# Query and key rows laid out in DRAM by pair of batches, with mask, ones and zero rows in blocks of 28

## What is computed

```python
query = seq2 + b_self
key = jnp.concatenate([seq1 + b_prev, seq2 + b_self], 1)
value = jnp.concatenate([seq1, seq2], 1)
q = (query @ Wq + bq).reshape(b, l2, H, DH).transpose(0, 2, 1, 3)
k = (key @ Wk + bk).reshape(b, l1 + l2, H, DH).transpose(0, 2, 1, 3)
...
score_prev = jnp.einsum('bhqd,bhkd->bhqk', q, k[:, :, :l1]) * SCALE
score_self = (q * k[:, :, l1:]).sum(-1, keepdims=True) * SCALE
mask = jnp.arange(l1)[None, :] < seq_len1[:, None]
score_prev = jnp.where(mask[:, None, None, :], score_prev, -jnp.inf)
score = jnp.concatenate([score_prev, score_self], -1)
weights = jax.nn.softmax(score, axis=-1)
```

## Time and profile before

| | |
|---|---|
| median of three runs | 500.7 us (499.92 to 501.67) |
| the profiled execution's own time | 500.33 us |
| its span, first to last instruction | 497.1 us |
| PE busy | 450.9 us (91%) |
| DVE, ACT, POOL busy | 344.3, 267.4, 191.7 us |
| mean granted TensorE clock | 0.943 |
| moved by DMA | 37.31 MB in 44730 packets |
| span's shares in the chain that ended last | PE 59%, DVE 11%, DMA 8%, SP's queue 8% |

### The profile page before, as it was taken

How to read it: one execution, slowest core, us unless ns; L and a number is a source line. 1 busy time by engine, 2 the same in 40 slices (tenths; PEclk the granted TensorE clock), 3 DMA queues, 4 the chain that set the end, 5 groups by cost and what they waited for, 6 DMA issues and landing times.

```text
span 497.1 us, 7804 instructions
## 1 busy us (share of the span) xinstructions
PE 450.9 (91%) x2278; PEld 328.2 (66%) x2278; DVE 344.3 (69%) x634; ACT 267.4 (54%) x544; POOL 191.7 (39%) x187
## 2 busy tenths in 40 slices
PE   6889899789999999999999999999997879978795
PEld 2667678567787887777788776887884434434442
DVE  5398567586777789677778967776875655766562
ACT  2457657465464664546466454646555434545463
POOL 4456676882132533113253311333773121222220
PEclk9689989899999999999999999999999785989889
DMA  5324333220004011000401000032107266455620
GB/s 152 112 79 112 122 86 112 79 67 1 2 7 125 3 63 42 0 0 6 123 2 62 21 1 0 7 104 65 61 22 195 64 176 180 141 168 167 179 74 22
DMA packets 44730, 37.31 MB, mean 75 GB/s; under 512 B 4216, under 2 KB 39196, under 8 KB 44700
## 3 DMA queue, kind: packets, MB, share of 16 engines
q1 hardware_dynamic: 43248, 36.64, 25.4%
q0 software_dynamic: 1024, 0.26, 0.3%
q10 hardware_dynamic: 432, 0.10, 0.1%
HBM read 26.07 MB, written 10.66 MB: 74 GB/s over the span
## 4 chain that ended last, share of the span: by engine, by line
PE 59%; DVE 11%; DMA 8%; SPq 8%; issue 5%; ACT 5%; POOL 3%; ACTq 0%; DVEq 0%
PE acc_ps L550 6%; SPq L460 5%; PE g_ps L550 5%; PE g_ps L552 5%; PE g_ps L551 5%; PE acc_ps L552 5%; PE acc_ps L551 5%; DVE act_lo L1103 4%; DMA w_raw<-in_L_cond_Wu 4%; PE u_ps L550 4%; PE u_ps L552 4%; PE u_ps L551 4%; DVE act_p L1099 3%; PE st_ps L718 3%; PE pv_ps L730 3%
## 5 line engine op out<-in xcount | busy, mean ns | idle before, releaser
L837 ACT ACTIVATE act_p<-g_ps 128x512 f32<-128x512 f32 x144 | 86.1, 598 | 135.4 <-PE g_ps L552 120.2
L1099 DVE TENSOR_TENSOR act_p<-act_p,u_ps 128x512 f32<-128x512 f32 x144 | 98.5, 684 | 72.9 <-PE u_ps L552 45.3
L1103 DVE TENSOR_TENSOR act_lo<-act_p,act_hi 128x512 fp32r<-128x512 f32 x144 | 121.9, 846 | 0.2 <-ACT act_hi L842 0.2
L1305 POOL TENSOR_TENSOR xg_lo<-xg,xg_hi 128x512 fp32r<-128x512 f32 x35 | 50.2, 1433 | 149.4 <-ACT xg_hi L847 149.4
L842 ACT ACTIVATE act_hi<-act_p 128x512 fp32r<-128x512 f32 x144 | 89.8, 624 | 4.8 <-DVE act_p L1099 4.7
L550 PE MATMUL acc_ps<-act_hi,w_split 128*128 128x512 f32 x144 | 62.1, 431 | 15.7 <-DVE act_lo L1103 15.6
L933 ACT ACTIVATE probs_t<-st_ps 128x512 f32<-128x512 f32 x64 | 38.2, 597 | 47.6 <-PE st_ps L718 47.5
L550 PE MATMUL g_ps<-x_hi,w_split 128*128 128x512 f32 (+1 forms) x144 | 58.6, 407 | 1.4 <-DVE x_lo L1128 1.4
L551 PE MATMUL g_ps<-x_lo,w_split 128*128 128x512 f32 (+1 forms) x144 | 57.7, 400 | 0.0
L552 PE MATMUL g_ps<-x_hi,w_split 128*128 128x512 f32 (+1 forms) x144 | 57.6, 400 | 0.0
L550 PE MATMUL u_ps<-xg_hi,w_split 128*128 128x512 f32 x144 | 57.1, 397 | 0.0
(11 more groups left out here) (147 smaller groups left out, 715.9 us busy)
## 6 DMA issues: line engine op xcount, KB each, us to landing
k_blocks<-k_rows SPq DMA_DIRECT2D x32, 96.0 KB
q_plain<-q_rows SPq DMA_DIRECT2D x8, 384.0 KB
q_blocks<-q_rows SPq DMA_DIRECT2D x32, 96.0 KB
k_plain<-k_rows SPq DMA_DIRECT2D x8, 384.0 KB
v_both<-v_d SPq DMA_DIRECT2D x8, 272.0 KB, 3.6
w_raw<-in_L_cond_Wg SPq DMA_DIRECT2D x8, 256.0 KB, 2.9
w_raw<-in_L_cond_Wu SPq DMA_DIRECT2D x8, 256.0 KB, 3.1
w_raw<-in_L_cond_Wd SPq DMA_DIRECT2D x8, 256.0 KB, 2.9
```

Of the source, the lines that this page charges most:

```text
L837: activation(act_p[k % 3][:], g_ps[k % 3][:], ACT.Silu).then_inc(silu_done, 1)
L1099: tt(act_p[k % 3][:], act_p[k % 3][:], u_ps[k % 3][:], ALU.mult).then_inc(prod_done, 1)
L1103: tt(act_lo[k % 3][:], act_p[k % 3][:], act_hi[k % 3][:].bitcast(F32), ALU.subtract).then_inc(act_lo_done, 1)
L1305: tt(xg_lo[e % 3][:], xg[:].rearrange("p b s -> p (b s)"), xg_hi[e % 3][:].bitcast(F32), ALU.subtract)\
```

## The change

The two DRAM tensors become (pair, 112 rows, 4, 256): a pair of batches lies together, and within it four blocks of 28 rows, of which 24 are as before, row 24 is the mask (keys) or ones (queries), and 25 to 27 are zero (for keys; for queries too, behind the ones). Each store of `store_rows` becomes two DMAs, one for each pair, of 128 pieces of 1 KB. Two DMAs of constants (512 and 384 KB, DRAM to DRAM) and four mask DMAs in place of one come behind the first tile. The block tiles put the groups j outermost, so that each block load is 28 partitions of one contiguous 4 KB, and each plain load 112 partitions of 4 KB. The loads of lines 466, 477 and 519 go away. A pair takes 13 DMAs. The matmuls of lines 619 and 718 contract over 112 and 114 rows in place of 97 and 99 and read their columns in steps of 4 KB in place of 1 KB.

```diff
-            def store_rows(dst, tok, places):
+            def store_rows(dst, t, places):
 
-                of_place = dst[0:ROW_MASK].rearrange("(j s r) i n -> j s (r i) n", j=GJ, s=3)
                 his, lo = places
-                for s in his:
-                    sp.dma_start(of_place[:, s, :, tok], rows_hi[:].bitcast(F32)).then_inc(rows_stored, 16)
-                sp.dma_start(of_place[:, lo, :, tok], rows_lo[:].bitcast(F32)).then_inc(rows_stored, 16)
+                for rows, s in [(rows_hi, s) for s in his] + [(rows_lo, lo)]:
+                    for m in range(TB // PAIR):
+                        to = dst[t * (TB // PAIR) + m].rearrange("(j x) i n -> j x i n", j=GJ)[:, s * DH:(s + 1) * DH]
+                        sp.dma_start(to.rearrange("j r i n -> j (r i) n"),
+                                     rows[:, m * PAIR * S:(m + 1) * PAIR * S].bitcast(F32)).then_inc(rows_stored, 16)
...
+            for rows, first in ((q_rows, 0), (k_rows, 1)):
+                to = rows.rearrange("p (j x) i n -> p j x (i n)", j=GJ)[:, :, BLOCK_MASK + first:BLOCK_ROWS]
+                sp.dma_start(to.rearrange("p j x n -> p j (x n)"),
+                             a["row_pads"][first:].rearrange("x n -> (x n)").unsqueeze(0).unsqueeze(0)
+                             .to_broadcast([NP, GJ, (BLOCK_ROWS - BLOCK_MASK - first) * GI * PAIR * S])).then_inc(pads_stored, 16)
             sp.wait_ge(mask_stored, 16)
-            sp.dma_start(k_rows[ROW_MASK:], mask_row.rearrange("b s -> (b s)").unsqueeze(0).unsqueeze(0)
-                         .to_broadcast([1, GI, B * S])).then_inc(later_stored, 16)
+            for j in range(GJ):
+                sp.dma_start(k_rows[:, BLOCK_ROWS * j + BLOCK_MASK],
+                             mask_row.rearrange("(p b) s -> p (b s)", b=PAIR).unsqueeze(1).to_broadcast([NP, GI, PAIR * S]))\
+                    .then_inc(later_stored if j == 0 else mask_stored, 16)
...
-            def load_blocks(dst, src, tok, semaphore):
+            def load_blocks(dst, src, p, semaphore):
 
                 for j in range(GJ):
-                    r = slice(3 * DH * j, 3 * DH * (j + 1))
-                    sp.dma_start(dst[r, :, j].bitcast(F32), src[r, :, tok]).then_inc(semaphore, 16)
+                    r = slice(BLOCK_ROWS * j, BLOCK_ROWS * (j + 1))
+                    sp.dma_start(dst[r, j].bitcast(F32).rearrange("r i n -> r (i n)"),
+                                 src[p, r].rearrange("r i n -> r (i n)")).then_inc(semaphore, 16)
+
+            def load_plain(dst, src, p, semaphore):
+                sp.dma_start(dst[0:ROW_MAX].bitcast(F32).rearrange("r i n -> r (i n)"),
+                             src[p].rearrange("r i n -> r (i n)")).then_inc(semaphore, 16)
...
-                mm((s_ps[i % 2] if bank is None else bank)[:], q_plain[n // 2 % 2][0:ROW_MASK + 1, i, half(n)],
-                   k_blocks[n // 2 % 2][0:ROW_MASK + 1, i, :, half(n)], start=True, stop=True).then_inc(s_written, 1)
+                mm((s_ps[i % 2] if bank is None else bank)[:], q_plain[n // 2 % 2][0:ROW_MAX, i, half(n)],
+                   k_blocks[n // 2 % 2][0:ROW_MAX, :, i, half(n)], start=True, stop=True).then_inc(s_written, 1)
```

More of the change, by code:

```diff
@@ L33 @@
 GI, GJ = 4, 4
-ROW_MASK = 3 * DH * GJ
-ROW_MAX = ROW_MASK + 1
+BLOCK_MASK = 3 * DH
+BLOCK_ROWS = BLOCK_MASK + 4
+ROW_MAX = BLOCK_ROWS * GJ
 Q_SLOTS, K_SLOTS = ((0, 2), 1), ((0, 1), 2)
@@ L46 @@
 NP = B // PAIR
+ROW_STORES = 16 * 3 * TB // PAIR
 NEXT_SLOT = {18: ("side", 0), 20: ("query", 0), 22: ("natural", 0), 24: ("natural", 1), 26: ("natural", 2),
@@ L91, in dram @@
             return nc.dram_tensor(name, shape, F32, kind="Internal").ap()
-        q_rows = dram("q_rows", (ROW_MASK, GI, B * S))
-        k_rows = dram("k_rows", (ROW_MASK + 1, GI, B * S))
+        q_rows = dram("q_rows", (NP, ROW_MAX, GI, PAIR * S))
+        k_rows = dram("k_rows", (NP, ROW_MAX, GI, PAIR * S))
         mask_row = dram("mask_row", (B, S))
@@ L246, in build @@
         mask_stored = sem("mask_stored")
+        pads_stored = sem("pads_stored")
         dif_step, z_step, gate_step, small_cast = sem("dif_step"), sem("z_step"), sem("gate_step"), sem("small_cast")
@@ L393, in later_stores @@
                 sp.wait_ge(aux_drained, n + 3)
-                store_rows(k_rows, bass.ds(t * N, N), K_SLOTS)
+                store_rows(k_rows, t, K_SLOTS)
                 sp.wait_ge(aux_drained, n + 4)
@@ L453, in _ @@
             later_stores(NT - 2)
-            def load_blocks(dst, src, tok, semaphore):
+            def load_blocks(dst, src, p, semaphore):
                 for j in range(GJ):
-                    r = slice(3 * DH * j, 3 * DH * (j + 1))
-                    sp.dma_start(dst[r, :, j].bitcast(F32), src[r, :, tok]).then_inc(semaphore, 16)
-            def load_first(p, m):
[L464 to L469, removed]
-            def load_second(p, m):
[L473 to L478, removed]
+                    r = slice(BLOCK_ROWS * j, BLOCK_ROWS * (j + 1))
[4 more added lines that the diff above has]
+                             src[p].rearrange("r i n -> r (i n)")).then_inc(semaphore, 16)
+            def load_first(p, m):
+                load_blocks(k_blocks[m % 2], k_rows, p, first_loaded[m % 2])
+                load_plain(q_plain[m % 2], q_rows, p, first_loaded[m % 2])
+            def load_second(p, m):
+                load_blocks(q_blocks[m % 2], q_rows, p, second_loaded[m % 2])
+                load_plain(k_plain[m % 2], k_rows, p, second_loaded[m % 2])
             def load_v(p, m):
@@ L508, in step @@
                     load_x3(p + 2, m)
-            sp.wait_ge(rows_stored, 16 * 3 * (2 * NT - 1))
+            sp.wait_ge(rows_stored, ROW_STORES * (2 * NT - 1))
             sp.wait_ge(later_stored, 16 * (1 + 2 * (NT - 1)))
+            sp.wait_ge(mask_stored, 16 * GJ)
+            sp.wait_ge(pads_stored, 32)
             for m in range(2):
@@ L530, in _ @@
             step(-1, 1, out=False, x3=False)
-            sp.wait_ge(rows_stored, 16 * 3 * 2 * NT)
+            sp.wait_ge(rows_stored, ROW_STORES * 2 * NT)
             sp.wait_ge(later_stored, 16 * (1 + 2 * NT))
@@ L718, in scores_t @@
                 mm(st_ps[i % 2][:], k_plain[n // 2 % 2][0:ROW_MAX + 2, i, half(n)],
-                   q_blocks[n // 2 % 2][0:ROW_MAX + 2, i, :, half(n)], start=True, stop=True).then_inc(st_written, 1)
+                   q_blocks[n // 2 % 2][0:ROW_MAX + 2, :, i, half(n)], start=True, stop=True).then_inc(st_written, 1)
             def weigh(b, n, i):
@@ L820, in first_step @@
                 else:
-                    wait(act, rows_stored, f * 96 - 48)
+                    wait(act, rows_stored, (2 * f - 1) * ROW_STORES)
                     activation(rows_hi[:], aux_ps[:], ACT.Identity, bias=cols[:, 0:1]).then_inc(aux_rounded, 1)
@@ L830, in later_step @@
                     act.wait_ge(aux_written, n + 1)
-                    act.wait_ge(rows_stored, 48 * (2 * NT - 1) if isinstance(t, int) and t == NT - 1 else t * 96 + 96)
+                    act.wait_ge(rows_stored, (2 * NT - 1) * ROW_STORES if isinstance(t, int) and t == NT - 1 else t * (2 * ROW_STORES) + 2 * ROW_STORES)
                     activation(rows_hi[:], aux_ps[:], ACT.Identity, bias=cols[:, 1:2]).then_inc(aux_rounded, 1)
@@ L1171, in split_max @@
                 own = self_score[:, b].rearrange("p (i j) -> p i j", i=GI)
-                part = neg_max[n % 2][:].rearrange("p c (i j) -> p c i j", i=GI)
+                part = neg_max[n % 2][:].rearrange("p c (j i) -> p c i j", i=GI)
                 dve.wait_ge(max_done, b * GI + GI)
@@ L1420, in shape_constants @@
         "key_pos": np.tile(np.arange(S, dtype=np.float32), (B, 1)),
+        "row_pads": np.repeat(np.float32([1, 0, 0, 0]), GI * PAIR * S).reshape(BLOCK_ROWS - BLOCK_MASK, GI * PAIR * S),
     }
```

15 lines of the change are left out of this document (6 added, 9 removed).

## The result

The changed kernel takes 507.13 us (median of 4, 506.16 to 508.39) against 500.7 us for the kernel before, a ratio of 1.0129 with a 95% interval of 1.0089 to 1.0168. It is slower by 1.3%; I had forecast 495.3 us and a range up to 500.5 us. A second comparison gave 507.67 us and 1.0128 (1.0072 to 1.0184). All ratios and intervals here leave out executions that ran in a second, slower state at a lower granted clock, such as one of 519.98 us of the kernel before. The profiled execution took 507.86 us.

The account below looks back on a forecast made before the run. The prediction took SP's issuing queue to bound the even part of phase 2. It summed 500.33 + 2.4 (stores) - 0.4 (start of phase 2) - 7.0 (pairs) = 495.3 us, with a range of 491.0 to 500.5 us.

Parts of the forecast that it names:

- The bound: Even part of phase 2: SP's issuing queue, 13.31 us a pair, bounds it, not the transfers; PE's own pace is 10.65 us.
- The issue of a block load: SP's queue in phase 2: 0.74 us in place of 0.79 us, bounds 0.33 and 0.90 us.
- signs of being wrong: Among them: weight loads landing over 13 us, block issues leaving 0.7 to 0.8 us, matmuls growing, pair above 12 us.
- the store term: First tile: 1 KB pieces lengthen each store drain by 1.2 us, twice on the chain, +2.4 us.
- What is late next: Batches 6 to 14: the queue at 11.25 us barely remains the bound; 44.4 us in place of 51.38, 7.0 us gained.
- the rival of cheap issues: SP's queue in phase 2: block issues at 0.33 us make PE the bound, 8.8 us gained, 493.5 us; chance 0.25.
- Start of phase 2: Load of values 0.5 us earlier, batch 3's maximum rows later, batch 4's wait gone; batch 4 starts 0.4 us earlier.
- The clock: Phase 2 pairs: the falls of PE's clock were counted on to go with the waits.
- the clock rival: Phase 2 pairs: remaining short waits still lower the clock, four pairs take 49.0 us, 500.0 us in all; chance 0.12.
- The slower rival: Store drains: 1 KB pieces cost as much as 2 KB ones, 8.2 us more each drain, 517.4 us; chance 0.10.
- Pads, masks, bytes, matmuls: Behind the first tile and in phase 2: extra DMAs, 16% more bytes, more rows and other strides all cost nothing.
- the dear rival: SP's queue in phase 2: block issues at 0.90 us, step 12.65 us, 2.8 us gained, 499.5 us; chance 0.11.

Follow-up runs that it names:

- a4: Changed kernel with two unused elements behind each 256 in block and plain tiles, so loads move 1 KB pieces; 494.52 us, ratio 0.9906 to the kernel before.
- b1: Changed kernel with each block load cut by partitions into two of 14, pieces still 4 KB; 495.42 us, ratio 0.9962 to the kernel before.
- a1: Kernel before with each row store alone cut into two DMAs of 1 KB pieces; 503.5 us, ratio 1.0005.
- c3: Changed kernel with the two unused elements in the block tiles alone, plain loads in 4 KB pieces; 492.53 us, ratio 0.9821 to the kernel before.
- b2: Changed kernel with the second half of a step's loads held until the next batch's maximum rows landed; 494.76 us, ratio 1.0011 to the kernel before.
- c2: Changed kernel with both the padded block tiles and SP's wait before the second half of a step's loads; 501.5 us, ratio 1.0007 to the kernel before.

## Why the prediction was wrong

- *The bound.* Right as far as it went: SP's queue paced the pairs. With it gone the wait for `k_plain` of batches 8, 10 and 12 went too.
- *The issue of a block load.* I took 0.74 us with 0.33 us as the lower end; it is 0.33 to 0.36 us. That is one of the signs of being wrong that I had named. The term was mis-sized, by giving partitions and engine count the price that the shape has: with four pieces for a partition the issue is 0.81 us (a4), with one 0.33 us, at the same 28 partitions; and 14 partitions cost as much as 28 (b1). What the Trainium skill ("DMA: Bandwidth & Descriptors", section on why a DMA increments its semaphore by 16) says of missing increments showed no price here. With 0.81 us, dearer than my 0.74 us, a4 came out at 494.5 us, near the forecast of 495.3 us. That is luck in part: the store term was 2.4 us too high, and from batch 6 to batch 14 a4 gained 3.3 us (48.1 us) where I had summed 7.0 us.
- *What is late next.* This is the step that failed. I summed 3 x 11.25 + 10.65 = 44.4 us for four pairs; they took 57.2 us, with 17.8 us of waits for the maximum rows in the whole of phase 2. I let PE's own 10.65 us follow the queue's 11.25 us, in the forecast and in the rival of cheap issues alike, and wrote of the bytes that "the transfers lie beside PE". The share of 0.54 was a mean under the old pace. I asked what each load waits for, not which other transfer the loads then get in the way of. The row for it was in my hands: batch 3 had already waited 2.14 us for its maximum rows behind the key store. I priced that once, at the start of phase 2, and did not carry it to the other batches. In the changed kernel it also happens in batches 1, 5, 7, 9 and 11. The rival that I priced at 493.5 us was the one whose condition came true, and it gave 507 us.
- *Start of phase 2.* I forecast 0.4 us gained and the end of batch 4's wait for `k_plain`. From the first memset to batch 6 the changed kernel took 56.9 us in place of 50.6 us (56.6 and 53.1 us in the second traces). Batch 1 waited 3.88 us and batch 5 2.57 us for their maximum rows, and batch 4's wait for `k_plain` grew from 1.12 us to 3.00 us. So about as much is lost here as in the four pairs behind it. The burst delays the maximum rows here too; why batch 4's load lands later was not tested.
- *The clock.* I counted on the falls going with the waits. With the new waits the clock of the stretch is 0.84 (0.87 in the second trace) in place of 0.90. But the second trace of the kernel before has 0.82 there with few waits, so these runs do not show that the new waits lowered it. The condition that I set for the clock rival, waits that stay, was met by waits that I had not thought of.
- *The stores.* +2.4 us forecast, nothing measured (a1: 1.0005). As twice as many pieces drained in the same time, a piece of 1 KB costs about half of one of 2 KB in a drain; the 55 ns from the earlier trace rows were those of loads among other pieces. The slower rival built on them did not come.
- *Pads, masks, bytes, matmuls.* Nothing that shows, as forecast: phase 1 is as long as before, and a matmul of 114 rows takes 0.47 to 0.50 us like one of 99 rows. The 16% more bytes are no cause by themselves, since a4, b1 and c3 carry them too.
- *The signs that I named.* "The pair stays above 12 us with no wait on a load in it" is what happened: from batch 6 (432.27) to batch 8 (448.27) it took 16.0 us, and the wait in it was for the maximum rows.
- *Slips in the sums.* They changed nothing that was decided. 0.79 us and 0.07 us, times 28/24, make 1.00 us and not 0.90 us; at 1.00 us the dear rival comes to about 501.9 us. Cheap issues save 8 x 0.46 us against the present issue and not 8 x 0.41 us, so the step is 8.1 us; PE stays the bound at 10.65 us. The measured 507.1 us lies outside a range up to 501.9 us too.

## What to carry to other kernels

A queue that is slow to issue is also a brake on its transfers. Before you make it faster, list the small transfers that are sent while its loads are in flight and ask how long they would stand behind all of the loads at once; if one of them is on the path, keep the pace (a4, b1, c3) or hold back half of the loads (b2). One of the two is enough: both together (c2) lost the gain. Sending the small one first was not tried. And a share of DMA time, like any mean, holds only for the order that it was measured under.

## What was not expected of the hardware

- The issue of a DMA with 28 partitions takes 0.81 us with four pieces of 1 KB for a partition and 0.33 us with one of 4 KB. A 14-partition one of the second form takes 0.33 us, and one of 112 partitions 0.32 to 0.37 us.
- Ten idle instructions ahead of each DMA on SP's queue cost no time that the trace shows (four loads within 1.60 us with and without).
- Loads to four groups of 28 partitions and plain loads drained at 193 GB/s, the same bytes in four loads to 112 partitions at 260 GB/s.
- A DMA of 8 KB took 6.3 us to land when it was issued into a burst of 1.8 MB, its packets spread among those of the burst; from POOL's and from ACT's queue alike the slowest took over 8 us, against 1.7 us in the quickest case.
